# Shared expert of a mixture-of-experts layer: three 128-column blocks in place of four of 96, five groups ahead of the routed experts, fifteen pieces among them

## The chip, the cores and the metric

The kernel runs on one core of one Trainium2 chip. The metric is the device time of one execution in microseconds. The kernel before takes 2819.9 us, the median of three runs (2819.66 to 2824.02).

## The reference, cut to what matters

The kernel computes an attention layer, a mixture-of-experts (MoE) layer, a state-space scan and a second MoE layer, on 4096 tokens of width 256 in float32. The change lies in the MoE layer, which is executed twice with the same weights:

```python
logits = x @ router_w.T                  # 64 experts, the best 8 of each token
xb = x_buf[:E * C].reshape(E, C, -1)     # up to C=128 rows gathered for each expert
h = silu(einsum('ecd,edf->ecf', xb, w_gate)) * einsum('ecd,edf->ecf', xb, w_up)   # F = 192
y = einsum('ecf,efd->ecd', h, w_down)
routed = segment_sum(y[safe] * weight, tok)
gu = x @ ws_gate_up                      # shared expert: every token, [256, 384]
sg, su = gu[:, :192], gu[:, 192:]
return routed + silu(sg) * su @ ws_down  # ws_down: [192, 256]
```

The shared expert is the last three lines. It needs no routing result; the routed experts do.

## The kernel before, in words

`ffn` runs two phases. `phase_route` normalizes the tokens, computes the logits, picks the experts, writes the table of normalized rows to memory and keeps their transpose in `xnT_all`. Meanwhile SyncE issues the loads of the shared weights (`load_shared`, L1011) and of the first 14 experts.

`phase_experts` (L1320) then has two stages.

*Ahead of the experts.* VectorE searches the lists of rows for each expert (sixteen index searches at L1535, then L1537 to L1553, with a small DMA at L1408 and a transpose on TensorE at L1659 in between), which ends in `ids_ready`. Beside it the shared expert is computed for the first `AHEAD = 4` of eight groups of 512 tokens. For each group TensorE makes four gate and up products of 96 columns (L1622, two matmuls each, every float32 matmul shows as two instructions), ScalarE takes each out of its bank (SiLU or copy, L1490), GpSimd multiplies gate by up (L1438), TensorE makes two down products of the group before (L1612), ScalarE copies them out (L1482), and GpSimd adds them to `x_sb` (L1429). After the last group TensorE's queue holds: the first down product of that group, which waits for GpSimd's multiplies; the wait for the lists; the transpose of L1659; the second down product. GpSimd's queue holds the multiplies of the last group, the adds of the group before it, the wait for `ids_ready`, seven gathers, the adds of the last group.

*The experts.* For each of 64 experts, in a software pipeline: GpSimd gathers the expert's rows by an indirect DMA (L1445, eight buffers `xg`); TensorE transposes them (L1671), makes gate and up in three blocks of 128 columns (L1695) and the down product of the expert before (L1679); ScalarE copies the transpose (L1515) and makes the SiLU (L1525, L1526); VectorE multiplies (L1589, L1591) and weighs the result (`weigh`, L1560); GpSimd scatters it with an accumulating indirect DMA into one of two sums in memory (L1453). SyncE loads the weights of expert n when the down product of expert n - 14 is done (L1411, L1020 to L1023). GpSimd's queue alternates: the gather of expert n + 7, then the scatter of expert n - 1. These are its waits:

```python
def gather(n):  pool.wait_ge(y_ready, n - XR + 1)                  # L1444, XR = 8
def scatter(n): pool.wait_ge(y_ready, n + 1)                       # L1450
                pool.wait_ge(summed[n % 2], 16 * (n // 2))         # L1452
```

So gather and scatter that stand beside each other need the same result of VectorE, and a scatter needs that the scatter two before it has landed, since both add into the same sum.

The other four groups of the shared expert are cut into six pieces each (four gate and up products, two down products), and one piece stands at every second expert from the second on (`piece_at`, L1400), on TensorE between the gate and up of expert n and the down product of expert n - 1 (L1698). VectorE multiplies SiLU (in SBUF) by up (in its bank, L1574) and adds the down products to `x_sb` (L1580); a piece comes before `weigh` in VectorE's queue (L1593).

The phase ends when every scatter has landed (L1473). The first layer is followed by the state-space stage, the second by `phase_merge`, which adds the sums and stores the output.

Of the kernel before, what the change touches and what calls it, by code (L numbers as in the profile page):

```python
# [11 lines left out]
ALU = mybir.AluOpType  # L12
# [3 lines left out]
P = 128  # L16
# [981 lines left out]
class ExpertWeights:  # L998
# [321 lines left out]
def phase_experts(nc, tag, x_sb, ident, order, xnT_all, table, sums, expert_weights):  # L1320
# [12 lines left out]

    AHEAD = 4
    AMONG = N - AHEAD
    PIECES = 2 * FC + 2
    FIRST, APART = 1, 2
    with ExitStack() as ctx:
# [13 lines left out]
        s_wgu, s_wd = expert_weights.shared_gate_up, expert_weights.shared_down  # L1352
        s_gu = m.sb("s_gu", [FP, 2, 2 * FC, GROUP])
        s_hh = m.sb("s_hh", [FP, 2, FC, GROUP])
        s_y = m.sb("s_y", [P, 2, 2 * D])
# [9 lines left out]
        pI = m.ps("pI", [P, 2, BANK])  # L1365
        s_bank = [pX[0:FP, 0, :], pX[0:FP, 1, :], pG[0:FP, 0, :], pG[0:FP, 1, :]]

# [11 lines left out]
        s_added = m.sem("s_added")  # L1379
        q_gate = m.sem("q_gate")  # L1380
        q_up = m.sem("q_up")
        q_silu = m.sem("q_silu")
        q_hh = m.sem("q_hh")
# [31 lines left out]
        def _(pool):  # L1415
# [16 lines left out]
            def shared(n, s, turn, ahead):  # L1432
                for c in range(FC):
                    pool.wait_ge(s_out, v(n * 4 + (c + 3)))
                    if not early(n, 2):

                        pool.wait_ge(s_down, v(n * 2 - 2))
                    pool.tensor_tensor(s_hh[:, s, c, :], s_gu[:, s, c, :], s_gu[:, s, FC + c, :], ALU.mult)\  # L1438
                        .then_inc(s_hh_ready, 1)
                if not early(n, 1):  # L1440
                    shared_add(n - 1)
# [34 lines left out]
        def _(act):  # L1476
# [7 lines left out]
            def shared(n, s, turn, ahead):  # L1484
                for f in range(2 * FC):
                    act.wait_ge(s_gated, v(n * 4 + (f + 1)))
                    if not early(n, 2):

                        act.wait_ge(s_hh_ready, v(n * 2 - 2))
                    act.activation(s_gu[:, s, f, :], s_bank[f], ACT.Silu if f < FC else ACT.Copy).then_inc(s_out, 1)  # L1490
                    if f % 2 and not early(n, 1):
                        shared_y(n - 1, f // 2)
            for n in range(AHEAD):
# [4 lines left out]
            def piece(g, i):  # L1498

                if i not in (0, 2):  # L1500
                    return
                c = i // 2
                act.wait_ge(q_gate, 2 * g + c + 1)
                if g < 2:
                    act.wait_ge(s_hh_ready, 2 * AHEAD)
                else:
                    act.wait_ge(q_hh, 2 * (g - 2) + c + 1)
                act.activation(s_gu[:, g % 2, c, :], pI[0:FP, 0, :], ACT.Silu).then_inc(q_silu, 1)

# [21 lines left out]
        def _(dve):  # L1531
# [31 lines left out]
            def piece(g, i):  # L1563

                at = AHEAD + g
                if i in (1, 3):
                    c = i // 2
                    dve.wait_ge(q_silu, 2 * g + c + 1)
                    dve.wait_ge(q_up, 2 * g + c + 1)
# [4 lines left out]
                    dve.tensor_tensor(s_hh[:, g % 2, c, :], s_gu[:, g % 2, c, :], pI[0:FP, 1, :], ALU.mult)\  # L1574
                       .then_inc(q_hh, 1)
                if i >= 2 * FC:
                    h = i - 2 * FC
                    dve.wait_ge(q_down, 2 * g + h + 1)
                    rows = x_sb[:, at * 2 + HT * h:at * 2 + HT * h + 2, :]
                    dve.tensor_tensor(rows, rows, pI[:, h, :].rearrange("p (t d) -> p t d", t=2), ALU.add)\  # L1580
                       .then_inc(q_added, 1)

            dve.wait_ge(padded, 2)
            for n in range(EXPERTS):
                q = n % 2
                dve.wait_ge(silu_ready, 2 * n + 2)
                if n >= 2:
                    dve.wait_ge(down, n - 1)
                dve.tensor_tensor(hh[0:H, q, :, :].rearrange("p c n -> p (c n)"), sg[H:P, q, 0:2 * CAP],  # L1589
                                  pG[H:P, q, CAP:3 * CAP], ALU.mult).then_inc(hh_ready, 1)  # L1590
                dve.tensor_tensor(hh[H:P, q, 0, :], sg[0:H, q, 2 * CAP:3 * CAP], pG[0:H, q, 2 * CAP:3 * CAP],  # L1591
                                  ALU.mult).then_inc(hh_ready, 1)
                if piece_at(n):  # L1593
# [7 lines left out]
        def _(pe):  # L1601
            pe.wait_ge(expert_weights.shared_in, 32)

            def shared_down(n, s, h):
# [4 lines left out]
                for q in range(2):  # L1609
                    for c in range(FC):  # L1610
                        at = (2 * h + q) * P
                        mm = pe.matmul(pY[:, h, q * D:(q + 1) * D], s_hh[:, s, c, at:at + P], s_wd[:, c, :],  # L1612
                                       start=(c == 0), stop=(c == FC - 1))
                mm.then_inc(s_down, 1)

            def shared(n, s, turn, ahead):
                for f in range(2 * FC):
                    if not early(n, 1):

                        pe.wait_ge(s_out, v(n * 4 + (f - 3)))  # L1620
                    for c in range(DC):
                        mm = pe.matmul(s_bank[f], s_wgu[:, c, f * FP:(f + 1) * FP],  # L1622
                                       xnT_all[:, c, bass.ds(v(n * GROUP), GROUP)],
                                       start=(c == 0), stop=(c == DC - 1))
                    mm.then_inc(s_gated, 1)
                    if f % 2 and not early(n, 1):
                        shared_down(n - 1, (s + 1) % 2, f // 2)
            def piece(g, i):

                at = (AHEAD + g) * GROUP  # L1630
                if i < 2 * FC:
                    c = i // 2
                    if i == 0:
                        pe.wait_ge(ids_ready, 1)
                    if i < 2 and g > 0:
                        pe.wait_ge(q_added, 2 * (g - 1) + i + 1)
                    if i == 2:
                        pe.wait_ge(q_silu, 2 * g + 1)
                    if i == 3:
                        pe.wait_ge(q_hh, 2 * g + 1)  # L1640
                    f = c + FC * (i % 2)
                    for k in range(DC):
                        mm = pe.matmul(pI[0:FP, i % 2, :], s_wgu[:, k, f * FP:(f + 1) * FP], xnT_all[:, k, at:at + GROUP],
                                       start=(k == 0), stop=(k == DC - 1))
                    mm.then_inc(q_up if i % 2 else q_gate, 1)
                else:
                    h = i - 2 * FC
                    pe.wait_ge(q_hh, 2 * g + 2)
                    for q in range(2):
                        for c in range(FC):  # L1650
                            mm = pe.matmul(pI[:, h, q * D:(q + 1) * D], s_hh[:, g % 2, c, (2 * h + q) * P:(2 * h + q + 1) * P],
                                           s_wd[:, c, :], start=(c == 0), stop=(c == FC - 1))
                    mm.then_inc(q_down, 1)
# [7 lines left out]

            pe.wait_ge(s_out, 4 * AHEAD)
            pe.wait_ge(s_y_ready, 2 * AHEAD)
# [766 lines left out]
```

## Time and profile before

| | |
|---|---|
| median of 3 runs | 2819.9 us (2819.66, 2819.9, 2824.02) |
| the profiled execution | 2823.65 us, its span 2821.7 us |
| mean granted TensorE clock | 0.925 |
| busy: TensorE, VectorE, ScalarE, GpSimd | 85%, 80%, 60%, 34% of the span |
| first MoE layer, expert phase | from about 1596 to 1865 us of the span |
| second MoE layer, expert phase | from about 2515 to 2783 us of the span |

The profile's busy shares are means over stages with different limits, so the rows below are read by stretch. A view of the timeline gives the start, the duration, the engine, the line and, in brackets, the idle time before an instruction and what ended it; "issue" there means that nothing that the profile shows was waited for. Tiles of the first layer's expert phase begin with f1e, of the second with f2e.

### The profile page before, as it was taken

The numbers are of one execution on the slowest core, as the hardware profiler recorded it, in microseconds if no ns is written. First come the engines' busy times: TensorE is split into PE (matmuls) and PEld (weight loads), VectorE is DVE, ScalarE is ACT, GpSimd is POOL, SyncE is SP. The second block draws the span as 40 slices with busy tenths as digits, with TensorE's granted clock in tenths as the row PEclk, the third lists the DMA queues.
The fourth block names the chain that finished last, engine by engine and source line by source line (L and its number), as shares of the span: only waits on it lengthen the run. The fifth ranks groups of instructions, "written<-read, shape, count | busy, mean of one in ns | idle before, by whom it ended". The sixth has DMA issues, their size and how long they took to land. (4 is left out here: it accounts for less than half of the span.)

```text
span 2821.7 us, 45555 instructions
## 1 busy us (share of the span) xinstructions
PE 2386.1 (85%) x14814; PEld 1060.6 (38%) x14814; DVE 2258.6 (80%) x3705; ACT 1691.3 (60%) x3462; POOL 961.9 (34%) x729
## 2 busy tenths in 40 slices
PE   8898999999999999999986799917476676679991
PEld 5322222222222222222225478812122222357881
DVE  7898999999999999999924844428799999785443
ACT  3347888888888888888881433306556556443330
POOL 4500000000000000000020277772499999426772
PEclk9879999999999999999997799957799999879996
DMA  4505111111111111111145469981234333245997
GB/s 152 145 24 177 43 34 50 50 36 40 50 50 36 40 50 50 32 44 50 28 132 186 142 162 270 234 124 28 55 112 113 105 112 110 85 142 153 272 239 204
DMA packets 255163, 293.69 MB, mean 104 GB/s; under 512 B 39120, under 2 KB 210448, under 8 KB 254928
## 3 DMA queue, kind: packets, MB, share of 16 engines
q1 hardware_dynamic: 213664, 235.09, 28.7%
q0 software_dynamic: 33104, 46.42, 8.9%
q10 hardware_dynamic: 8160, 9.32, 1.0%
q8 instruction: 115, 1.88, 0.3%
q14 instruction: 120, 0.98, 0.1%
HBM read 223.35 MB, written 66.75 MB: 103 GB/s over the span
## 5 line engine op out<-in xcount | busy, mean ns | idle before, releaser
L746 DVE TENSOR_REDUCE att_mx<-att_pR 128x1 f32<-128x512 f32 x2048 | 1266.2, 683 | 32.7 <-PE att_pR L786 32.7
L729 ACT ACTIVATE att_probs<-att_pS 128x512 f32<-128x512 f32 x2048 | 1064.0, 603 | 230.1 <-PE att_pS L816 229.9
L833 PE MATMUL att_pA<-att_probs,att_vh 128*17 128x512 f32 x4096 | 539.1, 598 | 12.6 <-ACT att_acc_sb L710 12.2
L816 PE MATMUL att_pS<-att_q,att_k 64*128 64x512 bf16 x1344 | 458.4, 379 | 0.6 <-DMA att_q<-att_nmT 0.4
L2299 PE MATMUL sc_pY<-sc_hc,all_ident 128*128 128x512 f32 x512 | 261.1, 634 | 126.9 <-DVE sc_hc L2256 102.8
L2165 POOL TENSOR_TENSOR sc_bh<-ssm_du,sc_b 128x1024 f32<-128x1024 f32 x128 | 297.7, 2358 | 8.9 <-DVE sc_hc L2256 4.7
L673 POOL TENSOR_TENSOR att_neg<-att_mx,att_minus 128x16 f32<-128x16 f32 x32 | 7.1, 221 | 842.4 <-DVE att_mx L754 842.4
L786 PE MATMUL att_pR<-head_k,head_q 64*128 64x512 bf16 x704 | 257.7, 403 | 14.3 <-PEq L72 7.4
L816 PE MATMUL att_pS<-head_q,head_k 64*128 64x512 bf16 (+1 forms) x1408 | 263.6, 380 | 0.2
L816 PE MATMUL att_pS<-att_qs,att_ks 64*128 64x512 bf16 x1344 | 260.6, 377 | 0.3
L786 PE MATMUL att_pR<-att_ks,att_qs 64*128 64x512 bf16 x672 | 259.3, 386 | 0.0
L786 PE MATMUL att_pR<-att_k,att_q 64*128 64x512 bf16 x672 | 258.9, 385 | 0.4 <-DVE att_mx L746 0.4
L2246 DVE TENSOR_TENSOR_SCAN sc_bh<-sc_pD,sc_carry,sc_bh 128x1024 f32<-128x1024 f32 x96 | 222.3, 2341 | 1.7 <-ACT sc_bh L2212 1.7
L2299 PEld LDWEIGHTS sc_pY<-sc_hc,all_ident 128*128 128x128 f32 x512 | 91.8, 196 | 276.7 <-DVE sc_hc L2256 140.6
L786 PEld LDWEIGHTS att_pR<-att_ks,att_qs 64*128 64x128 bf16 x672 | 62.3, 93 | 334.7 <-DVE att_mx L746 311.5
L816 PEld LDWEIGHTS att_pS<-att_q,att_k 64*128 64x128 bf16 x1344 | 124.0, 93 | 89.4 <-ACT att_probs L729 15.8
L786 PEld LDWEIGHTS att_pR<-head_k,head_q 64*128 64x128 bf16 x704 | 66.3, 94 | 235.7 <-DVE att_mx L746 209.2
L666 POOL COPY att_vh<-all_v 128x256 f32<-128x256 f32 x32 | 12.6, 397 | 414.0 <-PE att_pA L833 414.0
L833 PEld LDWEIGHTS att_pA<-att_probs,att_vh 128*17 128x17 f32 x4096 | 69.0, 95 | 141.5 <-issue 76.9
L1453 POOL DMA_INDIRECT expert_sum<-f2e_y,f2e_ids x64 | 101.4, 1584 | 28.3 <-issue 13.2
L1453 POOL DMA_INDIRECT expert_sum<-f1e_y,f1e_ids x64 | 101.4, 1584 | 26.0 <-issue 18.4
L816 PEld LDWEIGHTS att_pS<-head_q,head_k 64*128 64x128 bf16 (+1 forms) x1408 | 85.4, 94 | 62.1 <-ACT att_probs L729 7.2
(320 smaller groups left out, 3595.7 us busy)
## 6 DMA issues: line engine op xcount, KB each, us to landing
sc_b<-scan_rows SPq DMA_DIRECT2D x128, 256.0 KB
f_wgu<-in_w_gate SPq DMA_DIRECT2D x128, 192.0 KB
f_wgu<-in_w_up SPq DMA_DIRECT2D x128, 192.0 KB
expert_sum<-att_zeros SPq DMA_DIRECT2D x4, 4224.0 KB, 21.2
f_wd<-in_w_down SPq DMA_DIRECT2D x128, 128.0 KB
sc_c<-scan_rows SPq DMA_DIRECT2D x40, 256.0 KB
head_q<-query_parts SPq DMA_DIRECT2D x132, 64.0 KB, 2.2
head_k<-key_parts SPq DMA_DIRECT2D x132, 64.0 KB, 2.2
```

The lines of the kernel that those rows point to most:

```text
L666: pool.tensor_copy(vh[s][:, :, 0:DK], src.rearrange("p n t d -> p (n t) d")).then_inc(v_in, 1)
L673: pool.tensor_tensor(neg[:, :], mx[:, :], minus[:, :], ALU.mult).then_inc(neg_ready, 1)
L729: act.activation(probs[:, k % (2 * HALF), :], bank(place(k)), ACT.Exp, scale=float(DK) ** -0.5).then_inc(expd, 1)
L746: dve.tensor_reduce(mx4[s][:, k // QC, k % QC:k % QC + 1], pR[:, (s + k) % 3, :], AX.X, ALU.max).then_inc(maxed, 1)
L786: pe.matmul(pR[:, (s + k) % 3, :], q[rows, t * P:(t + 1) * P], kk[rows, c * GROUP:(c + 1) * GROUP], start=True, stop=True).then_inc(row_sc ...
L816: mm = pe.matmul(bank(place(k)), kk[rows, t * P:(t + 1) * P], q[rows, c * GROUP:(c + 1) * GROUP], start=not half, stop=bool(half))
L833: mm = pe.matmul(pA[32 * c:32 * c + DK + 1, :], vh[s][:, t, :], probs[:, (HALF * g + j) % (2 * HALF), :], start=(t == 0), stop=(t == KT - ...
L1453: pool.indirect_dma_start(out=sums[n % 2][:, :], out_offset=bass.IndirectOffsetOnAxis(ap=ids[:, n:n + 1], axis=0), in_=y[n % R][:, :], in_ ...
L2165: pool.tensor_tensor(bh[k % H_RING][:, :, :], du[:, :, col(b, k)], b_sb[s][:, :].rearrange("p (a n) -> p a n", a=1).to_broadcast([P, DC, S ...
L2246: dve.tensor_tensor_scan(both, pD[:, k % D_RING, :, :].rearrange("p c n -> p (c n)"), both, 0.0 if k < STATES else carry[:, 0, n:n + 1], A ...
L2299: mm = pe.matmul(pY[:, c, :], ident[:, :], hc[hc_slot(k)][:, c, :], start=(n == 0), stop=(n == STATES - 1))
```

## The change

The 384 columns of gate and up are cut into three blocks of 128: gate 0 to 127, gate 128 to 191 beside up 0 to 63, and up 64 to 191. ScalarE sorts them into two tiles, `s_gate` and `s_up`, with one instruction for the first block and two of 64 partitions for each other block. The multiplies are one of 128 and one of 64 partitions, both from SBUF; the contraction of the down product is 128 + 64 in place of 96 + 96. A group takes six matmuls for gate and up in place of eight, and its two multiplies both wait for all three blocks. `AHEAD` goes from 4 to 5. The other three groups make 15 pieces of five a group, one at every third expert from the second on; the pieces use the two banks `pI` in turn. In VectorE's queue `weigh` now stands before the piece. `load_shared` issues three DMAs in place of two. The diff, cut:

```diff
-        self.shared_down = m.sb("s_wd", [FP, FC, D])
+        self.shared_down = m.sb("s_wd", [P, 2, D])
...
-        eng.dma_start(self.shared_down[:, :, :], self.io["ws_down"].rearrange("(c p) n -> p c n", p=FP))\
-            .then_inc(self.shared_in, 16)
+        for c, rows in enumerate((P, FF - P)):
+            eng.dma_start(self.shared_down[0:rows, c, :], self.io["ws_down"][c * P:c * P + rows, :])\
+                .then_inc(self.shared_in, 16)
...
-    AHEAD = 4
+    AHEAD = 5
     AMONG = N - AHEAD
-    PIECES = 2 * FC + 2
-    FIRST, APART = 1, 2
+    PIECES = BLOCKS + 2
+    FIRST, APART = 1, 3
...
+        def taken(q):
+
+            g, i = divmod(q, PIECES)
+            return (q_out, BLOCKS * g + i + 1) if i < BLOCKS else (q_added, 2 * g + i - BLOCKS + 1)
+
+        def block_out(act, s, b, bank, done):
+
+            if b == 0:
+                act.activation(s_gate[:, s, 0, :], bank, ACT.Silu).then_inc(done, 1)
+            if b == 1:
+                act.activation(s_up[0:P - REST, s, 0, :], bank[REST:P, :], ACT.Copy)
+                act.activation(s_gate[0:REST, s, 1, :], bank[0:REST, :], ACT.Silu).then_inc(done, 1)
+            if b == 2:
+                act.activation(s_up[P - REST:P, s, 0, :], bank[0:REST, :], ACT.Copy)
+                act.activation(s_up[0:REST, s, 1, :], bank[REST:P, :], ACT.Copy).then_inc(done, 1)
...
             def shared(n, s, turn, ahead):
-                for c in range(FC):
-                    pool.wait_ge(s_out, v(n * 4 + (c + 3)))
...
+                pool.wait_ge(s_out, BLOCKS * n + BLOCKS)
+                if n >= 2:
+                    pool.wait_ge(s_down, n * 2 - 2)
+                for c, rows in enumerate(K_ROWS):
+                    pool.tensor_tensor(s_hh[0:rows, s, c, :], s_gate[0:rows, s, c, :], s_up[0:rows, s, c, :], ALU.mult)\
                         .then_inc(s_hh_ready, 1)
...
-                if i in (1, 3):
...
+                if i == BLOCKS - 1:
+                    dve.wait_ge(q_out, BLOCKS * g + BLOCKS)
...
+                    for c, rows in enumerate(K_ROWS):
+                        dve.tensor_tensor(s_hh[0:rows, g % 2, c, :], s_gate[0:rows, g % 2, c, :],
+                                          s_up[0:rows, g % 2, c, :], ALU.mult).then_inc(q_hh, 1)
...
+                if n >= 1:
+                    weigh(n - 1)
                 if piece_at(n):
                     piece(*piece_at(n))
-                if n >= 1:
-                    weigh(n - 1)
...
             def shared(n, s, turn, ahead):
-                for f in range(2 * FC):
...
+                for b in range(BLOCKS):
+                    i = BLOCKS * n + b
+                    if i >= 4:
+                        pe.wait_ge(s_out, i - 3)
                     for c in range(DC):
...
+                        mm = pe.matmul(s_bank[i % 4], s_wgu[:, c, b * P:(b + 1) * P],
+                                       xnT_all[:, c, n * GROUP:(n + 1) * GROUP],
                                        start=(c == 0), stop=(c == DC - 1))
                     mm.then_inc(s_gated, 1)
-                    if f % 2 and not early(n, 1):
-                        shared_down(n - 1, (s + 1) % 2, f // 2)
+                    if b and n:
+                        shared_down(n - 1, (s + 1) % 2, b - 1)
```

## Rows read from the trace of the kernel before

**Rows 1.** Windows by stage: length, then each engine's busy us (instructions), TensorE's clock, DMA share, GB/s.

```profile
1654.40:1805.00 150.60, 150.60 (x947) 128.80 (x947) 65.09 (x153) 51.35 (x144) 118.30 (x92) 1.00 1.04 269
...
1846.60:1865.00 18.40, 0.00 (x0) 0.00 (x0) 0.00 (x1) 0.00 (x0) 7.78 (x5) 0.53 0.35 41
...
2572.90:2723.50 150.60, 150.60 (x947) 128.80 (x947) 65.09 (x153) 51.35 (x144) 117.04 (x92) 1.00 1.03 267
```

**Rows 2.** Timeline of TensorE, end of the first layer's pieces: start us, us, instruction.

```profile
1800.93 1.50 PE L1695 MATMUL f1e_pG<-f1e_xT,f_wgu 128*128 128x128 f32 x12
...
1805.09 1.50 PE L1695 MATMUL f1e_pG<-f1e_xT,f_wgu 128*128 128x128 f32 x12
...
1807.52 1.50 PE L1695 MATMUL f1e_pG<-f1e_xT,f_wgu 128*128 128x128 f32 x12
```

**Rows 3.** Timeline of GpSimd, first layer's experts.

```profile
1654.39 0.95 POOL L1445 DMA_INDIRECT f1e_xg<-token_table,f1e_ids  x1 [0.53 <-DVE f1e_y L1560]
...
1688.61 1.59 POOL L1453 DMA_INDIRECT expert_sum<-f1e_y,f1e_ids  x1 [0.30 <-issue]
...
1691.80 1.59 POOL L1453 DMA_INDIRECT expert_sum<-f1e_y,f1e_ids  x1 [0.30 <-issue]
...
1836.36 0.99 POOL L1445 DMA_INDIRECT f1e_xg<-token_table,f1e_ids  x1 [0.30 <-issue]
...
1855.84 1.55 POOL L1453 DMA_INDIRECT expert_sum<-f1e_y,f1e_ids  x1 [1.08 <-DMA expert_sum<-f1e_y,f1e_ids]
```

**Rows 4.** Timeline of GpSimd, second layer's experts.

```profile
2572.88 0.94 POOL L1445 DMA_INDIRECT f2e_xg<-token_table,f2e_ids  x1 [0.49 <-DVE f2e_y L1560]
...
2588.87 1.59 POOL L1453 DMA_INDIRECT expert_sum<-f2e_y,f2e_ids  x1 [1.85 <-DVE f2e_y L1560]
...
2754.03 0.99 POOL L1445 DMA_INDIRECT f2e_xg<-token_table,f2e_ids  x1 [0.30 <-DVE f2e_y L1560]
...
2773.49 1.55 POOL L1453 DMA_INDIRECT expert_sum<-f2e_y,f2e_ids  x1 [1.09 <-DMA expert_sum<-f2e_y,f2e_ids]
```

**Rows 5.** Waits of GpSimd, 1654 to 1840 us: us in total, times, longest.

```profile
POOL f1e_xg L1445 <- DVE f1e_y L1560: 10.4, 22, 0.5
```

**Rows 6.** Timeline of the stage ahead of the experts, first layer, start and end.

```profile
1596.45 6.44 PE L1622 MATMUL f1e_pX<-f_xnT_all,f_s_wgu 128*96 128x512 f32 x8 [6.62 <-PEq L72]
...
1606.16 3.60 PE L1622 MATMUL f1e_pX<-f_xnT_all,f_s_wgu 128*96 128x512 f32 x8
...
1609.59 1.89 PE L1612 MATMUL f1e_pY<-f_s_wd,f1e_s_hh 96*128 96x256 f32 x8
...
1616.48 3.60 PE L1622 MATMUL f1e_pX<-f_xnT_all,f_s_wgu 128*96 128x512 f32 x8
...
1635.61 0.59 ACT L1490 ACTIVATE f1e_s_gu<-f1e_pG 96x512 f32<-96x512 f32 x1 [1.12 <-PE f1e_pG L1622]
...
1636.28 1.40 POOL L1438 TENSOR_TENSOR f1e_s_hh<-f1e_s_gu 96x512 f32<-96x512 f32 x1 [0.45 <-ACT f1e_s_gu L1490]
...
1637.64 2.49 POOL L1429 TENSOR_TENSOR all_x<-all_x,f1e_s_y 128x512 f32<-128x512 f32 x2
...
1637.73 1.99 PE L1612 MATMUL f1e_pY<-f_s_wd,f1e_s_hh 96*128 96x256 f32 x8 [0.43 <-POOL f1e_s_hh L1438]
...
1638.51 1.76 DVE L1546 TENSOR_TENSOR f1e_slots<-f1e_firsts,f1e_later 64x128 f32<-64x128 f32 x1 [1.95 <-DMA f1e_later<-f1e_firsts]
...
1640.33 0.28 PE L1659 MATMUL f1e_pI<-all_ident,f1e_slots 64*128 64x64 f32 x1 [0.60 <-DVE f1e_slotf L1547]
...
1641.61 1.10 POOL L1445 DMA_INDIRECT f1e_xg<-token_table,f1e_ids  x1 [1.48 <-DVE f1e_ids L1553]
```

**Rows 7.** Timeline of SyncE's queue in the first layer's routing phase.

```profile
1546.25 0.49 SPq L1023 DMA_DIRECT2D f_wd<-in_w_down  x1
...
1552.39 0.90 SPq L1104 DMA_DIRECT2D token_table<-f1r_rows  x2
```

**Rows 8.** Groups of VectorE, 1640 to 1850 us: shapes, count, busy us, mean ns, idle before.

```profile
L1574 DVE TENSOR_TENSOR f1e_s_hh<-f1e_s_gu,f1e_pI 96x512 f32<-96x512 f32 x8 | 5.5, 683 | 2.7 <-issue 2.7
```

More of the change, by code:

```diff
@@ L1365, in phase_experts @@
         pI = m.ps("pI", [P, 2, BANK])
-        s_bank = [pX[0:FP, 0, :], pX[0:FP, 1, :], pG[0:FP, 0, :], pG[0:FP, 1, :]]
+        s_bank = [pX[:, 0, :], pX[:, 1, :], pG[:, 0, :], pG[:, 1, :]]
+        REST = FF - P
+        K_ROWS = (P, REST)
         ids_own = m.sem("ids_own")
@@ L1379, in phase_experts @@
         s_added = m.sem("s_added")
[L1380 to L1382 removed]
+        q_gated = m.sem("q_gated")
+        q_out = m.sem("q_out")
         q_hh = m.sem("q_hh")
@@ L1484, in shared @@
             def shared(n, s, turn, ahead):
-                for f in range(2 * FC):
[L1486 to L1490, printed above, removed]
-                    if f % 2 and not early(n, 1):
-                        shared_y(n - 1, f // 2)
+                for b in range(BLOCKS):
+                    i = BLOCKS * n + b
+                    act.wait_ge(s_gated, i + 1)
+                    if n >= 2:
+                        act.wait_ge(s_hh_ready, n * 2 - 2)
+                    block_out(act, s, b, s_bank[i % 4], s_out)
+                    if b and n:
+                        shared_y(n - 1, b - 1)
             for n in range(AHEAD):
@@ L1498, in piece @@
             def piece(g, i):
[L1500 to L1508, printed above, removed]
+                if i < BLOCKS:
+                    act.wait_ge(q_gated, BLOCKS * g + i + 1)
+                    if g < 2:
+                        act.wait_ge(s_hh_ready, 2 * AHEAD)
+                    else:
+                        act.wait_ge(q_hh, 2 * (g - 2) + 2)
+                    block_out(act, g % 2, i, pI[:, (PIECES * g + i) % 2, :], q_out)
             def copy_x(n):
@@ L1573, in piece @@
                         dve.wait_ge(q_down, 2 * (g - 2) + 2)
[L1574 to L1577, printed above, removed]
+                    for c, rows in enumerate(K_ROWS):
+                        dve.tensor_tensor(s_hh[0:rows, g % 2, c, :], s_gate[0:rows, g % 2, c, :],
+                                          s_up[0:rows, g % 2, c, :], ALU.mult).then_inc(q_hh, 1)
+                if i >= BLOCKS:
+                    h = i - BLOCKS
                     dve.wait_ge(q_down, 2 * g + h + 1)
                     rows = x_sb[:, at * 2 + HT * h:at * 2 + HT * h + 2, :]
-                    dve.tensor_tensor(rows, rows, pI[:, h, :].rearrange("p (t d) -> p t d", t=2), ALU.add)\
+                    dve.tensor_tensor(rows, rows, pI[:, (PIECES * g + i) % 2, :].rearrange("p (t d) -> p t d", t=2), ALU.add)\
                        .then_inc(q_added, 1)
@@ L1609, in shared_down @@
                 for q in range(2):
-                    for c in range(FC):
+                    for c, rows in enumerate(K_ROWS):
                         at = (2 * h + q) * P
-                        mm = pe.matmul(pY[:, h, q * D:(q + 1) * D], s_hh[:, s, c, at:at + P], s_wd[:, c, :],
-                                       start=(c == 0), stop=(c == FC - 1))
+                        mm = pe.matmul(pY[:, h, q * D:(q + 1) * D], s_hh[0:rows, s, c, at:at + P], s_wd[0:rows, c, :],
+                                       start=(c == 0), stop=(c == 1))
@@ L1614, in shared_down @@
                 mm.then_inc(s_down, 1)
             def shared(n, s, turn, ahead):
-                for f in range(2 * FC):
-                    if not early(n, 1):
-                        pe.wait_ge(s_out, v(n * 4 + (f - 3)))
+                for b in range(BLOCKS):
+                    i = BLOCKS * n + b
+                    if i >= 4:
+                        pe.wait_ge(s_out, i - 3)
                     for c in range(DC):
-                        mm = pe.matmul(s_bank[f], s_wgu[:, c, f * FP:(f + 1) * FP],
-                                       xnT_all[:, c, bass.ds(v(n * GROUP), GROUP)],
+                        mm = pe.matmul(s_bank[i % 4], s_wgu[:, c, b * P:(b + 1) * P],
+                                       xnT_all[:, c, n * GROUP:(n + 1) * GROUP],
@@ L1624, in shared @@
                                        start=(c == 0), stop=(c == DC - 1))
                     mm.then_inc(s_gated, 1)
-                    if f % 2 and not early(n, 1):
-                        shared_down(n - 1, (s + 1) % 2, f // 2)
+                    if b and n:
+                        shared_down(n - 1, (s + 1) % 2, b - 1)
             def piece(g, i):
[L1630 to L1645, printed above, removed]
+                at, q = (AHEAD + g) * GROUP, PIECES * g + i
@@ L1646, in piece @@
+                bank = pI[:, q % 2, :]
+                if q == 0:
+                    pe.wait_ge(ids_ready, 1)
+                if q >= 2:
+                    pe.wait_ge(*taken(q - 2))
+                if i < BLOCKS:
+                    for c in range(DC):
+                        mm = pe.matmul(bank, s_wgu[:, c, i * P:(i + 1) * P], xnT_all[:, c, at:at + GROUP],
+                                       start=(c == 0), stop=(c == DC - 1))
+                    mm.then_inc(q_gated, 1)
                 else:
-                    h = i - 2 * FC
+                    h = i - BLOCKS
@@ L1648, in piece @@
                     pe.wait_ge(q_hh, 2 * g + 2)
[L1649 to L1652, printed above, removed]
+                    for t in range(2):
+                        for c, rows in enumerate(K_ROWS):
+                            mm = pe.matmul(bank[:, t * D:(t + 1) * D],
+                                           s_hh[0:rows, g % 2, c, (2 * h + t) * P:(2 * h + t + 1) * P],
+                                           s_wd[0:rows, c, :], start=(c == 0), stop=(c == 1))
```

17 lines of the change are left out of this document (6 added, 11 removed).

## The prediction

> **What bounds the kernel now.** I read three views, in this order. First the windows by stage: in the 150 us in which the pieces run, TensorE is busy all the time in both layers, at full granted clock, GpSimd shows only 117 to 118 us, and the DMA engines carry 267 to 269 GB/s; but after the last product, from 1846.6 to 1865 us, TensorE and VectorE do nothing while GpSimd still issues five instructions [rows 1]. The engine that looks 80% busy ends last. Second, TensorE's timeline: an expert with a piece takes 4.16 us (1800.93 to 1805.09), one without 2.43 us [rows 2]. So a piece costs 1.73 us, and with one at every second expert TensorE needs 3.29 us an expert. Third, GpSimd's timeline: one gather and one scatter take 3.19 us from scatter to scatter, of which 0.60 us are two gaps of 0.30 us that wait for nothing shown [rows 3]. That cycle has no slack to give: it is 97% of TensorE's 3.29 us, and longer than the 2.43 us of an expert without a piece.
>
> How close the two are can be counted. From the gather of expert 8 to that of expert 63 there are 55 such pairs, 175.5 us at 3.19. The first layer takes 1836.36 - 1654.39 = 182.0 us [rows 3], the second 2754.03 - 2572.88 = 181.2 us [rows 4]. So GpSimd waits 6.5 and 5.7 us in all. In the first layer 22 gathers that wait for VectorE's result explain 10.4 - 22 x 0.30 = 3.8 us of it [rows 5]; the other 2.7 us, and nearly all of the second layer's 5.7 us, are scatters that wait for the scatter two before (one costs 1.85 - 0.30 = 1.55 us at 2588.87; the page names VectorE there, but the gather just ahead of it had needed the same result) [rows 4]. After the last gather come 19.5 us of scatters in both layers [rows 3, 4]. In the second layer GpSimd already bounds the experts, in the first it shares that with TensorE.
>
> **The change part by part.**
>
> *Fewer pieces among the experts.* A new piece of gate and up is again two matmuls of 512 columns, and one of down four of 256, so I keep 1.73 us; 24 pieces become 15. TensorE saves 9 x 1.73 = 15.6 us a layer and needs (3 x 2.43 + 1.73) / 3 = 3.01 us an expert, below GpSimd's 3.19. The saving goes into waiting for gathers. What GpSimd can gain are its waits for VectorE: 3.8 us in the first layer, some 0.2 us in the second. The scatters' waits stay and are the unknown of this part. A load of weights is 589,824 bytes (256 x 384 + 192 x 256 floats), and it follows the down products; at 3.01 in place of 3.29 us an expert the DMA engines are asked for 196 in place of 179 GB/s, beside the 90 GB/s that are left for gathers and scatters out of 269 [rows 1]: about 286. No row shows that load for long. The lower bound for these waits is none at all, 0 in both layers. For the upper I take a doubling of the second layer's figure, 11.4 us a layer. I take 6.5 us a layer: near the second layer's 5.7 us, since both layers are now paced by GpSimd as that one was, and a little above it for the heavier load. Then the 55 pairs take 182.0 us in each layer: nothing gained in the first, 0.8 us lost in the second.
>
> *A fifth group ahead.* Before, a group takes 1616.48 - 1606.16 = 10.32 us: four gate and up products of (1609.59 - 1606.16) / 2 = 1.715 us, and so two down products of 1.73 us [rows 6]. A new group takes 3 x 1.715 + 2 x 1.73 = 8.6 us. The first group has no down products and ran slowly: 9.71 us for 6.86 [rows 6]; I keep its excess of 2.85 us, so it ends at 1596.45 + 5.15 + 2.85 = 1604.45. The second group makes two blocks until 1607.9 and then wants the multiplies of the first. These now wait for all three blocks: 0.2 us until ScalarE starts, two outputs of 0.6 us [rows 6], two multiplies of 1.25 us (an add of 128 partitions takes 2.49 / 2, a multiply of 96 took 1.40 at its slowest, [rows 6]), 0.1 us between them, so 4.05 us after the block, at 1608.5. The second group ends 0.6 us late at 1613.7, the other three 8.6 us apart, the last at 1639.5. Its third block was done at 1637.75; its multiplies are ready at 1641.8. TensorE's queue holds the transpose of the lists behind the first of the last two down products, so that runs from 1641.8 to 1643.5 and the transpose then, in place of 1640.33 [rows 6]: 3.2 us later. The lists themselves are ready by about 1640.3 as before and no longer decide. GpSimd has ended its adds by 1641.8 + 2.5 = 1644.3, and the gather follows 1.28 us behind the transpose as it does now [rows 6], at 1644.8. Bounds: 0 if the fifth group hid under the index search, and 4 us if the multiplies take 1.40 us each and the clock falls while TensorE waits 2.3 us. I take 3.2 us, twice: 6.4 us.
>
> *ScalarE and VectorE among the experts.* Five outputs in place of two SiLU a group, 0.6 us each, lie beside TensorE's work on an engine that is busy 51 of 150 us [rows 1]; what follows there is the copy of a transpose that is needed an expert later. Putting `weigh` ahead of the piece brings a result forward by up to 0.7 us, to a GpSimd that is late. Nothing for either. VectorE's multiply changes its second input from a bank to SBUF. Its time was 0.68 us [rows 8], and 12 such multiplies are made in both layers. Whether they hold up GpSimd's gathers and scatters no row shows: between 0 and 12 x 0.68 = 8.2 us. I take 0: the nearest row, the compare of two SBUF tiles at 1638.51, ran beside GpSimd's adds and it was VectorE that took long, 1.76 us for 64 x 128, ending 0.14 us behind them [rows 6]. The Trainium skill's page "SBUF — State Buffer", section "Who interferes with whom", says that a VectorE instruction with two SBUF inputs contends with a GpSimd instruction that reads SBUF and that whoever comes first keeps the port. By that rule a multiply could block one GpSimd instruction for its length, and the sum would be up to 8.2 us higher. The trace's 1.76 us agrees with the rule as far as it goes, with GpSimd first.
>
> *The third DMA of `load_shared`.* It moves the first expert loads by about 0.6 us on SyncE's queue, which then idles from 1546.74 to 1552.39 [rows 7]. Nothing; without that idle time 0.6 us a layer.
>
> **Sum.** 6.4 us for the starts, 0 and 0.8 us for the experts: 7.2 us. On the profiled execution's 2823.65 us that is 2830.9; that execution lies 3.75 us above the median, so against 2819.9 us I forecast 2827 us. A difference of 0.2% is 5.6 us, about what a measurement can tell here.
>
> **The rivals.**
> - *TensorE's saving arrives.* If GpSimd could follow at 3.01 us, each layer would gain 15.6 us and lose 3.2: 2 x -12.4 = -24.8, so 2795 us. For it speaks the fully busy TensorE [rows 1]; against it the 3.19 us of a pair [rows 3] and five instructions of GpSimd behind TensorE's last.
> - *No change: the scatters stop waiting, or the fifth group is hidden.* With 1 us of waits in place of 6.5 in each layer the sum is 7.2 - 11 = -3.8 us, 2816; with a hidden fifth group it is 0.8 us, 2821. For the first: loads end earlier, and the last scatters before the phase's end run with few loads beside them. Against the second: the transpose's place in TensorE's queue, behind GpSimd's multiplies. Between them lie also cases of my own sum with 5 us of waits a layer, 4 us.
> - *The heavier load decides.* If scatters wait 11.4 us a layer, or VectorE's multiplies block GpSimd, it is 7.2 + 9.8 = 17 or 7.2 + 8.2 = 15 us: 2835 to 2837. It decides where a scatter regularly takes longer than the 6.4 us between it and the next into the same sum.
>
> **How the numbers follow.** My forecast, 6 to 11 us slower, 0.46; the heavier load 0.14; no measurable change 0.31; TensorE's saving, in full or in part, 0.09. So slower by over 0.2% 0.60, within 0.2% 0.31, faster 0.09. The range takes in the forecast, most of the case without a change and most of the heavier load: 2818 to 2836 us. The likeliest case alone is 2826 to 2831.
>
> **What would show it right or wrong.** In the new profile TensorE should wait for gathers (L1671's line) among the last third of the experts, GpSimd's pairs should stand at 3.19 us with waits only for scatters, no gather after the first few waiting for VectorE, the transpose of the lists should start 47 us after the first shared matmul in place of 43.9, and the last scatters should again take 19.5 us. The forecast is wrong if a pair takes clearly less than 3.19 us, if the first gather is not late, or if the scatters' waits disappear or double.

## The result, and the profile after

The changed kernel takes 2846.0 us (median of 4 runs, 2843.4 to 2848.3), the kernel before took 2820.8 us on the same chip: a ratio of 1.0083, with a 95% interval of 1.0071 to 1.0096. It is slower by 25 us, where 7 were forecast and 16 was the end of the range. The direction was right, and so was the reason that there would be no gain among the experts; the cost of the start was mis-sized by a factor of three.

The experts first, since the sum rested on them. The windows by stage of the changed kernel, for the stretches in which the pieces run, with the columns of [rows 1] (each begins with the gather of expert 8, as there):

```profile
1660.60:1811.20 150.60, 147.07 (x942) 124.06 (x941) 64.12 (x156) 57.25 (x157) 116.01 (x90) 1.00 1.03 273
2593.00:2743.60 150.60, 148.30 (x955) 126.03 (x953) 64.50 (x157) 58.28 (x160) 117.05 (x91) 1.00 1.05 279
```

TensorE is no longer busy all the time, and GpSimd issues about as much as before in the same length. GpSimd's timeline says why. The rows begin just ahead of the first gather:

```profile
1640.72 2.48 POOL L1456 TENSOR_TENSOR f1e_s_hh<-f1e_s_gate,f1e_s_up 128x512 f32<-128x512 f32 x2 [5.13 <-ACT f1e_s_up L1422]
1643.17 2.48 POOL L1448 TENSOR_TENSOR all_x<-all_x,f1e_s_y 128x512 f32<-128x512 f32 x2
1647.15 1.10 POOL L1463 DMA_INDIRECT f1e_xg<-token_table,f1e_ids  x1 [1.50 <-DVE f1e_ids L1569]
...
1660.64 0.94 POOL L1463 DMA_INDIRECT f1e_xg<-token_table,f1e_ids  x1 [1.24 <-DVE f1e_y L1576]
...
1701.18 1.59 POOL L1471 DMA_INDIRECT expert_sum<-f1e_y,f1e_ids  x1 [0.30 <-DVE f1e_y L1576]
...
1704.36 1.59 POOL L1471 DMA_INDIRECT expert_sum<-f1e_y,f1e_ids  x1 [0.30 <-issue]
...
1844.56 0.99 POOL L1463 DMA_INDIRECT f1e_xg<-token_table,f1e_ids  x1 [0.30 <-issue]
...
1863.95 1.55 POOL L1471 DMA_INDIRECT expert_sum<-f1e_y,f1e_ids  x1 [1.03 <-DMA expert_sum<-f1e_y,f1e_ids]
...
2579.88 1.12 POOL L1463 DMA_INDIRECT f2e_xg<-token_table,f2e_ids  x1 [1.90 <-DVE f2e_ids L1569]
...
2592.95 0.94 POOL L1463 DMA_INDIRECT f2e_xg<-token_table,f2e_ids  x1 [0.75 <-DVE f2e_y L1576]
...
2774.22 0.99 POOL L1463 DMA_INDIRECT f2e_xg<-token_table,f2e_ids  x1 [0.30 <-issue]
...
2793.48 1.55 POOL L1471 DMA_INDIRECT expert_sum<-f2e_y,f2e_ids  x1 [0.90 <-DMA expert_sum<-f2e_y,f2e_ids]
```

A pair still takes 3.18 us (1704.36 - 1701.18). From the gather of expert 8 to that of expert 63 the layers take 183.9 and 181.3 us, before 182.0 and 181.2 [rows 3, 4]; the last scatters take 19.4 and 19.3 us as before. What moved is the start. The first gather begins 54.5 us behind the first shared product, which starts at 1592.65; before it was 1641.61 - 1596.45 = 45.16 us [rows 6]. TensorE's timeline shows what stands ahead of it (L1637 is gate and up, L1627 down, L1670 the transpose of the lists; the first row, then all rows of one group ahead and the first of the next, then the end):

```profile
1592.65 6.18 PE L1637 MATMUL f1e_pX<-f_xnT_all,f_s_wgu 128*128 128x512 f32 x8 [5.75 <-PEq L72]
...
1611.15 3.70 PE L1637 MATMUL f1e_pG<-f_xnT_all,f_s_wgu 128*128 128x512 f32 x8
1614.69 2.48 PE L1627 MATMUL f1e_pY<-f_s_wd,f1e_s_hh 128*128 128x256 f32 x8
1617.09 1.98 PE L1637 MATMUL f1e_pX<-f_xnT_all,f_s_wgu 128*128 128x512 f32 x4
1618.91 2.48 PE L1627 MATMUL f1e_pY<-f_s_wd,f1e_s_hh 128*128 128x256 f32 x8
1621.32 1.98 PE L1637 MATMUL f1e_pX<-f_xnT_all,f_s_wgu 128*128 128x512 f32 x4
...
1643.26 2.79 PE L1627 MATMUL f1e_pY<-f_s_wd,f1e_s_hh 128*128 128x256 f32 x8 [1.53 <-POOL f1e_s_hh L1456]
1645.84 0.31 PE L1670 MATMUL f1e_pI<-all_ident,f1e_slots 64*128 64x64 f32 x1
```

A down product takes 2.40 us from start to start (1617.09 - 1614.69), where I had kept 1.73. A group takes 1621.32 - 1611.15 = 10.17 us, hardly less than the 10.32 of before [rows 6], though it has a quarter fewer gate and up products. So a fifth group is nearly a whole old group more, and the transpose comes 53.19 us behind the first shared product instead of 43.88 (53.09 instead of 43.63 in the second layer). The groups of TensorE's instructions by shape, 1600 to 1643 us, narrow it down (mean ns of one behind the busy time):

```profile
L1627 PE MATMUL f1e_pY<-f_s_wd,f1e_s_hh 64*128 64x256 f32 x32 | 11.1, 428 | 0.0
L1627 PE MATMUL f1e_pY<-f_s_wd,f1e_s_hh 128*128 128x256 f32 x32 | 10.5, 408 | 0.4 <-POOL f1e_s_hh L1456 0.4
```

The contraction over 192 rows is now made as 128 and 64, where it was 96 and 96. A down product goes through 128, 64, 128, 64 rows, and the gate and up products around it have 128: four changes of the number of rows in each, none before.

**The balance.** The span grows by 19.7 us. From the first shared product to the gather of expert 8: 1660.64 - 1592.65 = 67.99 us against 57.94, so +10.05, and in the second layer +9.74 (2592.95 - 2525.48 against 2572.88 - 2515.15). From there to gather 63: +1.95 and +0.12. Last scatters: -0.1 and -0.2. All that is elsewhere: -1.9. So the start carries it, in both layers alike. The medians differ by more, 25.3 us: the profiled execution of the kernel before took 2.9 us more than its median, that of the changed kernel 2.7 us less than its own. No rows show where these 5.5 us lie.

### The profile page after: what moved, and what is told of

Its sections match the earlier page's. It is cut to its first block and busy times, and to the rows that moved or that the text cites. A ratio compares the mean times of both kernels' runs of the same rounds, so it can differ in the third digit from the quotient of the medians.

```text
span 2841.4 us, 45471 instructions
## 1 busy us (share of the span) xinstructions
PE 2399.1 (84%) x14750; PEld 1045.5 (37%) x14750; DVE 2252.2 (79%) x3697; ACT 1712.1 (60%) x3498; POOL 972.6 (34%) x737
## 5 line engine op out<-in xcount | busy, mean ns | idle before, releaser
L833 PEld LDWEIGHTS att_pA<-att_probs,att_vh 128*17 128x17 f32 x4096 | 69.0, 95 | 141.8 <-issue 77.1
```

The lines of the kernel that those rows point to most:

```text
L833: mm = pe.matmul(pA[32 * c:32 * c + DK + 1, :], vh[s][:, t, :], probs[:, (HALF * g + j) % (2 * HALF), :], start=(t == 0), stop=(t == KT - ...
```

## The experiments

The theory (A): each change between a contraction of 128 rows and one of 64 costs TensorE time, about 0.2 us; that makes a group ahead as long as before, the fifth group sits in TensorE's queue ahead of the transpose, and GpSimd's pairs allow nothing back among the experts. The rivals: the product of 64 rows is slow in itself; the fifth group alone costs this, whatever its width; TensorE's work does bound the experts. Beside the first four runs below the kernel before took 2824.7 us, beside the other four 2824.9 us; each ratio is to those runs.

**Filled to 128 rows.** Weights and hidden values of the second part get 64 rows of zeros, so that every contraction has 128 rows.

```
+ pool.memset(s_wd[REST:P, 1, :], 0.0).then_inc(padded, 1)
+ pool.memset(s_hh[REST:P, :, 1, :], 0.0).then_inc(padded, 1)
...
- pe.matmul(..., s_hh[0:rows, s, c, at:at + P], s_wd[0:rows, c, :], ...)
+ pe.matmul(..., s_hh[:, s, c, at:at + P], s_wd[:, c, :], ...)
```

> The changed kernel with the second part of the down product's contraction filled up with zeros from 64 to 128 rows (in the shared expert's weights and activations), so that all its products have 128 rows. Theory A, each change of TensorE between products of 128 and of 64 rows costs some 0.2 us: a down product takes 1.73 us in place of 2.41, a group ahead 8.6 in place of 10.17, the transpose of the lists starts 47 us after the first shared matmul in place of 53.2, each layer gains about 6.1 us: 2834 us. Theory B, the start is late because of the fifth group and the place of the transpose whatever a product costs: transpose at 53, 2846 us.

Measured: 2835.4 us, a ratio to the kernel before of 1.0037 (1.0025 to 1.0049), against 1.0083 unfilled. TensorE's timeline, one group and the end, and then its groups by shape from 1603 to 1640 us:

```profile
1617.54 1.88 PE L1639 MATMUL f1e_pX<-f_xnT_all,f_s_wgu 128*128 128x512 f32 x4
1619.26 1.89 PE L1629 MATMUL f1e_pY<-f_s_wd,f1e_s_hh 128*128 128x256 f32 x8
1620.98 1.88 PE L1639 MATMUL f1e_pX<-f_xnT_all,f_s_wgu 128*128 128x512 f32 x4
...
1626.14 1.88 PE L1639 MATMUL f1e_pG<-f_xnT_all,f_s_wgu 128*128 128x512 f32 x4
...
1640.46 2.80 PE L1629 MATMUL f1e_pY<-f_s_wd,f1e_s_hh 128*128 128x256 f32 x8 [2.11 <-POOL f1e_s_hh L1458]
1643.19 0.36 PE L1672 MATMUL f1e_pI<-all_ident,f1e_slots 64*128 64x64 f32 x1
```

```profile
L1629 PE MATMUL f1e_pY<-f_s_wd,f1e_s_hh 128*128 128x256 f32 x64 | 15.2, 381 | 0.4 <-POOL f1e_s_hh L1458 0.4
```

More rows to multiply, and less time: a down product takes 1.72 us (1620.98 - 1619.26), one matmul instruction 381 ns in place of 408 and 428, a group 1626.14 - 1617.54 = 8.60 us. That is the figure of the prediction. A is shown as far as the group's length goes. The transpose starts 48.0 us behind the first shared product in both layers, where 47 was expected: it gained 5.2 and 5.1 us, not 6.1.

**The same products in another order.** 128, 64, 64, 128 rows, so two changes in a down product where there were four; no product is added, dropped or filled.

```
- for c, rows in enumerate(K_ROWS):
+ for c in (q, 1 - q):
+     rows = K_ROWS[c]
...
- start=(c == 0), stop=(c == 1))
+ start=(c == q), stop=(c != q))
```

> The changed kernel with the two parts of every second accumulation of the down product in the reverse order (128, 64, 64, 128 in place of 128, 64, 128, 64): the same products, two changes of rows in place of four. Theory A, the change costs: a down product takes about 2.0 us, a group ahead 9.4 us, the transpose starts about 49.6 us after the first shared matmul, 2839 us. Theory C, a product of 64 rows itself is slower: down product 2.41 us and transpose at 53.2 us as before this edit, 2846 us.

Measured: 2846.5 us, 1.0072 (1.0049 to 1.0094). TensorE's timeline:

```profile
1623.16 1.88 PE L1638 MATMUL f1e_pX<-f_xnT_all,f_s_wgu 128*128 128x512 f32 x4
1624.88 2.28 PE L1628 MATMUL f1e_pY<-f_s_wd,f1e_s_hh 128*128 128x256 f32 x8
1627.00 1.88 PE L1638 MATMUL f1e_pX<-f_xnT_all,f_s_wgu 128*128 128x512 f32 x4
...
1632.55 1.88 PE L1638 MATMUL f1e_pG<-f_xnT_all,f_s_wgu 128*128 128x512 f32 x4
```

A group takes 9.39 us. With eight changes a group it took 10.17, with none 8.60: (10.17 - 8.60) / 8 = 0.196 us a change, and (9.39 - 8.60) / 4 = 0.198. The cost goes with the changes; a product of 64 rows that was slow in itself would have cost the same in any order. Less of it arrived than expected: the transpose starts 50.9 and 50.7 us behind the first shared product, not 49.6, and so 2.3 us a layer earlier than in the changed kernel. The total doesn't show that gain: for both layers it is 0.17% of the time, less than the width of the interval.

**Four groups ahead in place of five,** unfilled, with 20 pieces (`AHEAD = 4`).

> The changed kernel with four groups ahead in place of five (20 pieces at every third expert). Theories A and B: one group of 10.17 us less ahead, so the lists decide again, the transpose starts 44.0 us after the first shared matmul, the experts are paced by GpSimd as in the changed kernel, 20.0 us a layer from the last gather to the last scatter unchanged: 2822 to 2826 us. Rival, the slower pieces or the spacing of the pieces among the experts cost too: above 2830 us.

Measured: 2827.7 us, 1.001 (0.9998 to 1.0022). TensorE's timeline at the end of the groups ahead:

```profile
1640.42 0.37 PE L1670 MATMUL f1e_pI<-all_ident,f1e_slots 64*128 64x64 f32 x1 [1.23 <-DVE f1e_slotf L1563]
```

The transpose waits for VectorE's lists again, not for products: 1640.42 - 1596.12 = 44.3 us behind the first shared product (44.6 in the second layer). In this kernel the fifth group is what makes the start late. Five further pieces a layer cost at most what the interval leaves, some 6 us in all; the stretch from gather 8 to gather 63 takes 179.9 and 182.6 us with them.

**The kernel before with a fifth group.** Blocks of 96 as before, and 18 pieces at every third expert.

```
- AHEAD = 4
+ AHEAD = 5
- FIRST, APART = 1, 2
+ FIRST, APART = 1, 3
```

> The kernel before with five groups ahead in place of four, its four products of 96 columns kept (18 pieces at every third expert). Theory A: a group of 10.32 us more, no changes of rows, the transpose 53 us after the first shared matmul in place of 43.9, 9 us a layer: 2839 to 2842 us, nearly the changed kernel's time, since there the changes of rows give back what the fourth product saved. If the fifth group were hidden: 2821 us.

Measured: 2838.7 us, 1.0046 (1.0029 to 1.0063). TensorE's timeline:

```profile
1647.67 2.00 PE L1612 MATMUL f1e_pY<-f_s_wd,f1e_s_hh 96*128 96x256 f32 x8 [0.29 <-POOL f1e_s_hh L1438]
1649.60 0.27 PE L1659 MATMUL f1e_pI<-all_ident,f1e_slots 64*128 64x64 f32 x1
```

The transpose stands 1649.60 - 1597.53 = 52.07 us behind the first shared product, 53.1 in the second layer: nearly where the changed kernel has it. So the changed kernel's wider blocks bought nothing ahead of the experts; their saving went into the changes of rows. Why this kernel's time is still some 0.4% (10 us) below the changed one's I can't place by rows: gather 8 comes 2.0 and 0.2 us earlier behind the first shared product, the rest of the experts is alike, and its profiled execution, 2845.5 us, was the slowest of its five.

**No pieces among the experts at all.** The kernel before with `AMONG = 0`: the shared expert of four of the eight groups of tokens is left out, 24 pieces of 1.73 us [rows 2] in each layer.

> The kernel before without the pieces of the shared expert among the routed experts: the shared expert of four of the eight groups of tokens is left out, which takes some 41 us a layer of products off TensorE. GpSimd theory (the experts are paced by the 3.19 us that GpSimd needs for one gather and one scatter): gather 8 to gather 63 still takes 178 to 182 us a layer, and the time falls by 0 to 8 us. Rival (TensorE paces the experts): the loop falls by 20 to 41 us a layer, the time by 40 to 80 us.

Measured: 2826.0 us, 1.0001 (0.9992 to 1.001). The windows from gather 8 to gather 63, with the columns of [rows 1]:

```profile
1652.50:1834.50 182.00, 153.24 (x1045) 131.81 (x1044) 68.89 (x174) 59.76 (x174) 141.78 (x110) 1.00 0.97 252
2573.70:2753.80 180.10, 154.80 (x1045) 133.16 (x1044) 69.58 (x177) 59.84 (x175) 141.81 (x111) 0.99 0.98 254
```

```profile
1654.40:1836.40 182.00, 182.00 (x1179) 158.92 (x1179) 79.82 (x190) 64.73 (x183) 141.84 (x111) 1.00 0.99 253
2572.90:2754.00 181.10, 181.10 (x1175) 158.12 (x1175) 79.83 (x190) 64.15 (x181) 141.78 (x110) 1.00 0.99 254
```

The second fence is the same view of the kernel before. TensorE has 134 and 130 instructions less and nothing else to do in their place, its busy time falls from 182 to 153 us in the first layer and from 181 to 155 us in the second, and the stretch takes 182.0 us as before (180.1 after 181.1 in the second), GpSimd busy 141.8 in all four. This is the strongest test of the prediction's first part: TensorE at 100% was not the bound. GpSimd at 78% was, because 110 gaps of 0.30 us that are counted as idle lie between its instructions [rows 3]; 141.8 + 33.0 = 174.8 us of the 182.0.

The run alone leaves a rival that the expectation doesn't name: the DMA engines are busy 97 to 99% of these stretches and carry the same 252 to 254 GB/s with and without the pieces. GpSimd's rows in the kernel before speak against it. From 1643 to 1650 us, ahead of the experts, where the DMA share is 0.46, a gather takes 0.95 us and its gap 0.30; behind the last gather, where the share is 0.35 [rows 1], a scatter takes 1.56 us and its gap, where it waits for nothing, 0.30. That makes a pair of 3.11 us with little DMA load, against 3.19. So the load is worth at most 0.08 us a pair, and beyond that the scatters' waits, some 7 us of the 182.

**The transpose ahead of both last down products,** in the filled kernel with five groups; nothing else moves.

```
- shared_down(AHEAD - 1, (AHEAD - 1) % 2, 0)
  pe.wait_ge(listed, 1)
...
+ shared_down(AHEAD - 1, (AHEAD - 1) % 2, 0)
  shared_down(AHEAD - 1, (AHEAD - 1) % 2, 1)
```

> The filled kernel with five groups, with the transpose of the lists put ahead of both last down products in TensorE's queue instead of between them. My theory (the transpose is late because the fifth group's products are queued before it): it moves up by one or two groups' down products to 43 to 46 us behind the first shared product (48.0 with the old place), but the first gather is then held by GpSimd's own multiplies and adds of the fifth group, so gather 0 comes at about 48 instead of 49.3: a gain of 1 to 1.5 us a layer, 2832 to 2834 on the scale where the filled kernel has 2835. Rival (TensorE's queue alone holds the start): gather 0 moves with the transpose, 3 to 5 us a layer, 2826 to 2829.

Measured: 2830.7 us, 1.0016 (1.0007 to 1.0025). GpSimd's timeline:

```profile
1639.99 2.48 POOL L1458 TENSOR_TENSOR f1e_s_hh<-f1e_s_gate,f1e_s_up 128x512 f32<-128x512 f32 x2 [3.65 <-ACT f1e_s_up L1422]
1642.43 2.48 POOL L1450 TENSOR_TENSOR all_x<-all_x,f1e_s_y 128x512 f32<-128x512 f32 x2
1645.08 1.10 POOL L1465 DMA_INDIRECT f1e_xg<-token_table,f1e_ids  x1 [0.17 <-issue]
```

The transpose now runs at 1640.34, 43.3 us behind the first shared product in place of 48.0, and the lists are ready at 1641.33; the first gather still starts only at 48.0 us (before this edit 49.3), right behind GpSimd's own multiplies and adds of the fifth group. In the second layer it moved from 49.4 to 46.9. So one wait takes the place of another, as my theory has it; the gain was larger than I wrote, 1.3 and 2.5 us against 1 to 1.5, and the time lies between the two ranges that I gave, below my theory's and above the rival's.

**Filled, four groups ahead.** The changed kernel with zeros in the second part and `AHEAD = 4`.

> The three blocks with the second part of the contraction filled with zeros to 128 rows, and four groups ahead of the experts again (20 pieces at every third expert). Theory A (the late start is TensorE's queue of groups ahead, 8.6 us a group without changes of rows): four groups instead of five bring the lists' transpose from 48.0 us behind the first shared product to about 42, where the slots end (42.0 and 41.5 in the filled kernel with five groups); gather 0 at 43.3 to 44, against 45.2 and 44.9 in the kernel before. The experts stay on GpSimd's 3.19 us a pair. That is 1 to 2 us a layer off the kernel before, less some 1.5 us in the second layer's stage of routes: 2817 to 2822 where the kernel before has 2821, a ratio of 0.999. Theory B (TensorE's columns bound the experts, so that 15 to 20 smaller pieces bring a gain of their own): a ratio of 0.99 or below.

Measured: 2822.3 us, 0.999 (0.9979 to 1.0001). VectorE's timeline, from the end of the index search on, in the unfilled kernel with four groups and then in this one:

```profile
1634.56 1.10 DVE L1553 TENSOR_SCALAR f1e_left<-f1e_where 128x128 f32<-128x128 uint32 x1
1635.69 1.19 DVE L1556 TENSOR_SCALAR f1e_upper<-f1e_left,f1e_half 128x128 f32<-128x128 f32 x1
1636.91 1.25 DVE L1558 SCALAR_TENSOR_TENSOR f1e_firsts<-f1e_left,f1e_upper 128x128 f32<-128x128 f32 x1
```

```profile
1637.18 0.23 DVE L1555 TENSOR_SCALAR f1e_left<-f1e_where 128x128 f32<-128x128 uint32 x1
1637.44 0.28 DVE L1558 TENSOR_SCALAR f1e_upper<-f1e_left,f1e_half 128x128 f32<-128x128 f32 x1
1637.76 0.29 DVE L1560 SCALAR_TENSOR_TENSOR f1e_firsts<-f1e_left,f1e_upper 128x128 f32<-128x128 f32 x1
```

The transpose starts 41.6 and 41.7 us behind the first shared product, 2.3 and 1.9 us earlier than in the kernel before, and 2.7 and 2.9 us earlier than in the unfilled one. The three rows explain these 2.7 us: they take 0.80 us in place of 3.54, and the first of them starts 38.44 us behind the first shared product in both kernels. GpSimd's last multiplies and adds of the shared expert in the unfilled kernel, and then, in this one, the first gather, which tells in brackets how long GpSimd had been done with them:

```profile
1633.03 2.48 POOL L1456 TENSOR_TENSOR f1e_s_hh<-f1e_s_gate,f1e_s_up 128x512 f32<-128x512 f32 x2 [5.23 <-ACT f1e_s_up L1422]
1635.47 2.53 POOL L1448 TENSOR_TENSOR all_x<-all_x,f1e_s_y 128x512 f32<-128x512 f32 x2
```

```profile
1641.69 1.10 POOL L1465 DMA_INDIRECT f1e_xg<-token_table,f1e_ids  x1 [4.55 <-DVE f1e_ids L1571]
```

In this kernel they are over at 1637.14, before the first of VectorE's three rows starts; in the unfilled kernel they run from 1633.03 to 1638.00, beside all three. I had expected that of the lists' compare alone. The rival, a gain of 1% from TensorE's columns, fell.

**The last adds on VectorE, the first piece at expert 4.** On top of the kernel just above; VectorE adds the last group ahead to x before its first expert.

```
- FIRST, APART = 1, 3
+ FIRST, APART = 4, 3
- shared_add(AHEAD - 1)
+ for h in range(2):
+     dve.wait_ge(s_y_ready, 2 * (AHEAD - 1) + h + 1)
+     ...
+     dve.tensor_tensor(rows, rows, s_y[:, h, :].rearrange("p (t d) -> p t d", t=2), ALU.add)
```

> As the run with four filled groups, and two more edits: the first piece waits for expert 4 instead of expert 1, and the last group's two adds to x go from GpSimd, where they stand between gathers 6 and 8, to VectorE ahead of the first expert. Theory A (GpSimd's queue and the first output y bound the start): the 12.5 to 12.8 us from gather 0 to gather 8 fall by up to 1.7 us in each layer, the rest stays; a ratio of 0.997 to 0.999 against the kernel before. Rival: gather 8 waits for the first y, which TensorE and ScalarE set, and neither edit touches that chain: 12.5 us stay, and the ratio is that of the run with four filled groups.

Measured: 2819.9 us, 0.9981 (0.9971 to 0.999): the only kernel here that is faster than the kernel before. GpSimd's timeline, gather 8 in both layers:

```profile
1652.94 0.95 POOL L1466 DMA_INDIRECT f1e_xg<-token_table,f1e_ids  x1 [2.38 <-DVE f1e_y L1579]
...
2568.71 0.95 POOL L1466 DMA_INDIRECT f2e_xg<-token_table,f2e_ids  x1 [1.71 <-DVE f2e_y L1579]
```

Gather 8 now waits 2.38 and 1.71 us for the first expert's result. From gather 0 it takes 12.8 and 11.8 us, against 12.9 and 12.7 without the two edits: the rival holds in the first layer, A's gain of 0.8 us shows in the second. Whether these edits or only the filled blocks with four groups make it faster is open, since the two intervals overlap.

## Why the prediction was right and wrong

- *What bounds the experts: right, and shown.* With no pieces at all the stretch from gather 8 to gather 63 takes 182.0 and 180.1 us. In the changed kernel no gather after expert 8 waits longer than 0.3 us, TensorE waits for gathers only from 1800 us on in the first layer (seven times, 5.7 us), and pairs stand at 3.2 us, all as forecast. TensorE's waits for gathers from 1660 to 1850 us (us in total, times, longest):

```profile
PE f1e_pX L1682 <- DMA f1e_xg<-token_table,f1e_ids: 5.7, 7, 1.1
```

  My 182.0 us a layer came out as 183.9 and 181.3. Over all kernels it lies between 179.9 and 183.9, changed loads and pieces or not, so the 2 us between the first layer's two values can't be told from that spread. Two points were off without harm. TensorE didn't share the bound in the first layer, whose stretch takes 182.0 us without pieces too. And of the 15.6 us a layer that I had TensorE save, its busy time in this stretch shows 5.9 (from 182.0 to 176.1 and from 181.1 to 175.2 us); in the filled kernel it shows 9.7, so part of the saving went into the changes of rows among the experts too.
- *The fifth group: the step of the prediction that failed is "A new piece of gate and up is again two matmuls of 512 columns, and one of down four of 256, so I keep 1.73 us".* It counted columns and left out that the rows change. A down product ahead of the experts takes 2.40 us in place of 1.73. From it came "3 x 1.715 + 2 x 1.73 = 8.6 us" for a group; measured 10.17, of which 8 changes at 0.196 us are 1.57. The delay of the start, 3.2 us in the sum, came out as 9.3 and 9.5: 4.1 and 4.4 in the filled kernel, and 5.2 and 5.1 more with the changes. By length alone four groups would add 4 x 1.57 = 6.3 us, and my sum 7.2 + 2 x 6.3 = 19.8 us, beside 19.7 us between the spans. That this agrees so closely is luck, since 6.3 is too much and 3.2 too little; with the longer products TensorE waits 1.53 us in place of 2.11 for GpSimd's last multiplies, which is part of the difference. The Trainium skill's page "TensorEngine Tiling (Array Packing)", section "Key Properties", says that changing the tiling mode drains TensorE; I didn't weigh it. The 0.196 us a change would agree with it if a contraction of 64 rows counts as another mode than one of 128; no run here shows that it does, or what TensorE does in that time, and so why a change costs stays open.
- *With equal rows the working nearly holds.* In the filled kernel the group takes the 8.60 us of the prediction, and the whole 10.7 us (2835.4 against 2824.7) where the sum had 7.2. The transpose is 4.1 and 4.4 us late, not 3.2: the last down product waits 2.11 us and then takes 2.73 us in place of 1.72, with a granted clock of 0.70 from 1640.4 to 1643.2, a mean between the levels of 1.2 and 2.4 GHz, where it was 1.00 from 1617.5 to 1626.1. That is about the upper bound of 4 us that I named and didn't take, and by the wait and the clock that I gave for it, though the multiplies took 1.24 us each and not 1.40. (The terms of the 4.05 us in that paragraph add up to 4.0; nothing hangs on it.)
- *The range* was built from bounds on waits and on the loads; the price of a matmul had none, because I took it as known from a row with another number of rows.
- *VectorE's multiply from two SBUF tiles: nothing seen, as taken.* In the changed kernel it takes 0.68 us as before [rows 8], and GpSimd's pairs don't lengthen beside it:

```profile
L1589 DVE TENSOR_TENSOR f1e_s_hh<-f1e_s_gate,f1e_s_up 128x512 f32<-128x512 f32 (+1 forms) x6 | 3.8, 680 | 0.0
```

- *The third DMA: open, at most some 2 us.* The second layer's routing takes 67.8 us in the changed kernel and 66.1 before. All seven kernels with three DMAs take 67.1 to 68.1 us there; of the three with two DMAs two take 66.1 and 66.5, but the kernel without pieces 67.5. The first layer's, 65.2 to 67.5 us, shows no such order.
- *The rival of the heavier load fell:* 273 and 279 GB/s in place of 269 and 267, the pairs as before.

## What to carry to other kernels

When a contraction is cut anew, look at how many rows each matmul has and what the one before it had, not at columns alone: equal parts (96 and 96), or zeros up to 128, cost less here than 128 and 64 in turn: 1.73 and 1.72 us a down product against 2.40. Before you take work off an engine that is 100% busy, look for another whose cycle has only fixed gaps in it, and drop the work once to see whether the time moves. Work that is moved out of a loop with hidden time into the stretch ahead of it is paid as soon as it stands in one queue with what releases the loop, less what the release had to spare: 8.60 us of a filled group made the transpose 4.1 and 4.4 us late, 10.32 us of a group of the kernel before 8.2 and 9.5.

## What the runs showed of the hardware

A change between contractions of 128 and 64 rows costs TensorE about 0.2 us in float32, twice measured at 0.196 and 0.198 us; multiplying 64 rows of zeros instead makes the down product no longer than one of 96 and 96 rows, 1.72 us beside 1.73. And three small operations of VectorE, 0.23 to 0.29 us each alone, took 1.10 to 1.25 us beside GpSimd's multiplies and adds of 128x512, among them two with a single SBUF tile of full size as input; that was enough to move the lists' transpose by 2.7 us. In the prediction I had looked at the opposite direction alone, GpSimd held up by VectorE. Of that the traces show 0.13 us: in both layers of the kernel before, the multiply that starts together with VectorE's operation of L1542 takes 1.40 us where the others take 1.26 or 1.27 [rows 6].
